# A bias product on TensorE with 128 rows of contraction, 126 of them zeros, in place of two

## The chip, the cores and the metric

The kernel runs on one core of one Trainium2 chip. The metric is the device time of one execution in microseconds (us), lower is better. A core has TensorE (PE, matrix products; its weight loads are listed apart as PEld), VectorE (DVE), ScalarE (ACT), GpSimd (POOL) and SyncE (SP). Each runs its own instruction list in order and waits for the others on semaphores.

## The reference, cut to what matters

One layer: additive attention without a score matrix, then a mixture of experts. The part that the change touches is the end of the attention:

```python
wv = (pooled_k[:, None, :, :] * mixed_q.reshape(b, s, h, dh)).reshape(b, s, dm)
return wv @ Wt + bt + mixed_q        # mixed_q = hidden_states @ Wq + bq
...
x = x + _L0_attn_ref(_layernorm(x), ...)
x = x + _L0_ffn_ref(_layernorm(x), ...)
```

There are 2 batches of 2048 tokens, and 256 features per token. Since `pooled_k` is one vector per batch, the attention's output is, for each token, `xn @ M + c`, with one 256x256 matrix `M = Wq (diag(pooled_k) Wt + I)` and one row `c` of 256 numbers for the batch.

## The kernel before

The tokens lie in `x_sb` as 32 tiles of 128 tokens. The attention's last step, here called the projection, goes over 16 pairs of tiles: `project(q)` on TensorE for q = 0 to 15 (batch 0 has q = 0 to 7, batch 1 has q = 8 to 15). Each pair has one bank of `psU`, 128 partitions by 2 x 256 numbers, and gets 13 products:

- L599, four products: the high part of the normalised input (`xhigh`, stationary) by the high part of `M` (`mhl[:, 0]`), 256 columns each
- L603, four: the low part of the input (`xlow`) by the high part of `M`
- L608, four: the high part of the input by the low part of `M`
- L611, one: the bias row `c`. It is split into a high and a low row, `cpair`, which have the partitions 0 and 1; the stationary operand `one2` is two rows of ones. So this product has 2 rows of contraction, 128 output partitions and 2 x 256 moving columns (the same row twice, by a broadcast). It closes the accumulation.

All operands of these 13 products are of type fp32r. On VectorE `add_rows(q)` waits for the product L611 of pair q, adds the bank to `x_sb` (L1261) and takes the statistics of both tiles (L1264, L1265). After every fourth pair `second_moments_of` works out a variance (L1111 to L1124), GpSimd raises it to -1/2 (`zscale`, L424), and ScalarE (the last group: VectorE, L1281) writes normalised rows to `z_sb` (L891). TensorE transposes these (`turn_z`, L621), ScalarE copies them to `xT` (L928), and from there come the router's product (L632) and the first products of the expert part (`up`, L698, L700, L704, whose operand `xhl` is made by ScalarE at L945 and VectorE at L1290). The rest of the program, from about 105 us on, is the expert part.

The order of the work is written out by hand on each engine. TensorE's list has the second batch's pooling steps between the products of batch 0 (`fold_key` L500 and L504, `score` L519, `turn_max` L526, `spread_max` L532, `turn_probs` L540, `pool_rows` L548, `project_pooled` L567), and `turn_z` between those of batch 1. VectorE's list has the answering steps between its `add_rows`; L1216 writes `gk`, which `fold_key` reads. `bias_row(b)` (L1238 to L1240) writes `cpair` for batch b, and the first `project` of a batch waits for it. `cpair` and `one2` are SBUF tensors of 2 partitions. At its start VectorE fills 256 columns of `flat` (the trace calls it fold) with ones at L1296, for TensorE's opening products L757, and then waits for the first tile of x (L1133). `helpers` makes `one2` with one copy (L1165).

Of the kernel before, what the change touches and what calls it, by code (L numbers as in the profile page):

```python
# [19 lines left out]
ALU = mybir.AluOpType  # L20
ACT = mybir.ActivationFunctionType
F32 = mybir.dt.float32
F32R = mybir.dt.float32r
# [5 lines left out]
P = 128  # L29
D, KD = 256, 2  # L30
# [3 lines left out]
B, S = 2, 2048  # L34
# [36 lines left out]
C_HILO = C_ROW + 1  # L71
# [15 lines left out]
def build(nc, x, consts, attn, norm, bt, wpack, b1pack, b2pack, out):  # L87
    with ExitStack() as ctx:
        def sb(name, shape, dt=F32):
            return ctx.enter_context(nc.sbuf_tensor(name, shape, dt))  # L90
# [4 lines left out]
        def sem(name):  # L95
            return ctx.enter_context(nc.semaphore(name))
# [11 lines left out]
        cst = sb("cst", [P, C_ALL])  # L108
# [53 lines left out]
        flat = fold[:].rearrange("p a b k d -> p (a b k d)")  # L162
# [12 lines left out]
        with ExitStack() as early:  # L175
            z_sb = early.enter_context(nc.sbuf_tensor("z_sb", [P, NT, D], F32))
            att = early.enter_context(nc.sbuf_tensor("att", [P, A_ALL], F32))
            cpair = early.enter_context(nc.sbuf_tensor("cpair", [2, B, D], F32R))
            one2 = early.enter_context(nc.sbuf_tensor("one2", [2, P], F32R))
            stats = early.enter_context(nc.sbuf_tensor("stats", [P, NT, 6], F32))  # L180
            ssum, sdif, sm2, mean, var, vare, rstd, nmr = (
                early.enter_context(nc.sbuf_tensor(name, [P, NT], F32))
                for name in ("ssum", "sdif", "sm2", "mean", "var", "vare", "rstd", "nmr"))
            gk = early.enter_context(nc.sbuf_tensor("gk", [P, KD, B, 32], F32))
            pool_sb = early.enter_context(nc.sbuf_tensor("pool_sb", [P, B, KD, NH], F32))
# [17 lines left out]
        ones = cst[:, C_ONE:C_ONE + P]  # L203
# [21 lines left out]
        crow, chi = xin[0:2, 0, 0, 0:D], xin[0:2, 0, 1, 0:D]  # L225
# [39 lines left out]
        var_ready, rstd_ready, fill_ready = sem("var_ready"), sem("rstd_ready"), sem("fill_ready")  # L265
# [193 lines left out]
        def _(pe):  # L459
            mm = nc.tensor.matmul  # L460
# [125 lines left out]
            def project(q):  # L586
                before = [p for p in range(q) if proj_bank[p] == proj_bank[q]]
                if before:
                    pe.wait_ge(x1_ready, before[-1] + 1)
                b = 2 * q // (NT // B)  # L590
                if q % (NT // 4) == 0:
                    pe.wait_ge(m_ready[b], 1)
                pair = psU[:, proj_bank[q], :].rearrange("p (t n) -> p t n", t=2)
                n = q // 2
                cols = [slice((2 * q + tt) % 4 * P, ((2 * q + tt) % 4 + 1) * P) for tt in range(2)]
                pe.wait_ge(xhigh_ready, n + 1)
                for tt in range(2):
                    for k in range(KD):
                        mm(pair[:, tt, :], xhigh[b][:, n % 4, k, cols[tt]], mhl[:, 0, k, :], start=(tt == 0 and k == 0), stop=False)  # L599
                pe.wait_ge(xlow_ready, n + 1)  # L600
                for tt in range(2):
                    for k in range(KD):
                        mm(pair[:, tt, :], xlow[:, n, k, cols[tt]], mhl[:, 0, k, :], start=False, stop=False)  # L603
                if q % (NT // 4) == 0:
                    pe.wait_ge(m_low[b], 1)
                for tt in range(2):
                    for k in range(KD):
                        mm(pair[:, tt, :], xhigh[b][:, n % 4, k, cols[tt]], mhl[:, 1, k, :], start=False, stop=False)  # L608
                if q % (NT // 4) == 0:
                    pe.wait_ge(crow_ready[b], 1)  # L610
                last = mm(pair, one2[:, :], cpair[:, b:b + 1, :].to_broadcast([2, 2, D]), start=False, stop=True)  # L611
                last.then_inc(proj_ps, 1)

            def turn_z(q):
# [182 lines left out]
            mix(0)  # L797
            turn_pooled(1, 0)
            project(0)
            project_pooled(1, 0)  # L800
            project(1)
            fold_key(1)
            project(2)
            score(1, 1)
            project(3)
# [46 lines left out]
            for r in range(2):  # L852
                pe.wait_ge(logits_sb, r + 1)
                for i in range(4):
                    last = nc.tensor.transpose(psT[:, r, i * P:(i + 1) * P], lgT[:, r, i * P:(i + 1) * P], ident)
# [241 lines left out]
        def _(dve):  # L1097
            count = [0]

            def link(ins):  # L1100

                count[0] += 1
                ins.then_inc(dve_step, 1)
                dve.wait_ge(dve_step, count[0])

            V = nc.vector
# [20 lines left out]
            def stats_of(c):  # L1127
                if c >= 2:
                    dve.wait_ge(x_loaded[c], 16)
                for t in range(c * CH, (c + 1) * CH):  # L1130
                    if c < 2:
                        dve.wait_ge(first_loaded[t], 16)
                    last = V.bn_stats(stats[:, t, :], x_sb[:, t, :])  # L1133
                return last

            def first_moments(i):
                a, z = GRP[i]
                link(stats_of(z // CH - 1))
                moments(a, z, False, var_ready)
# [19 lines left out]
            def helpers():  # L1159
                link(V.tensor_reduce(own, ident.rearrange("p (g h) -> p h g", g=4), X, ALU.add))  # L1160
                V.tensor_copy(sel.rearrange("p (g h) -> p g h", g=4),
                              own.rearrange("p (o h) -> p o h", o=1).to_broadcast([P, 4, 32]))
                for n in range(KD):
                    V.tensor_scalar(bqrep[:, n, :], ones[:, 0:32], att[:, A_BQ + n:A_BQ + n + 1], None, ALU.mult)
                V.tensor_copy(one2[:], ones[0:2, :])  # L1165

            def row_max(b, r):

# [66 lines left out]
            def bias_row(b):  # L1235

                dve.wait_ge(crow_ps[b], 1)
                link(V.tensor_tensor(crow, psD[0:2, b, 0:D], bt_bc[0:2, :], ALU.add))  # L1238
                link(V.tensor_copy(chi.bitcast(F32R), crow))
                V.scalar_tensor_tensor(cpair[:, b, :], chi, cst[0:2, C_HILO:C_HILO + 1], crow,  # L1240
                                       ALU.mult, ALU.add).then_inc(crow_ready[b], 1)

            def mix_low(b):
# [50 lines left out]
                last.then_inc(xlo_ready, 1)  # L1294

            V.memset(flat[:, 0:256], 1.0).then_inc(fill_ready, 1)  # L1296
            stats_of(0)
            first_moments(0)
            stats_of(2)
# [6 lines left out]
            folded_query()  # L1306
            first_moments(2)
            helpers()
            row_max(0, 0)
            offsets(2)  # L1310
# [28 lines left out]
            mix_low(0)  # L1339
            dve.wait_ge(bt_loaded, 16)  # L1340
            bias_row(0)
            add_groups(1, 0)
            add_rows(0)
# [22 lines left out]
            second_moments_of(1)  # L1366
            mix_low(1)
            bias_row(1)
            z_offsets(1)
            add_rows(8)  # L1370
# [407 lines left out]
```

## Time and profile before

| | us |
|---|---|
| median of 3 runs | 724.13 |
| the runs | 722.74, 725.20, 724.13 |
| time of the profiled execution | 722.72 |
| its span, first to last instruction | 720.9 |

| engine | busy us | share of the span |
|---|---|---|
| TensorE, products | 703.4 | 98% |
| TensorE, weight loads | 587.1 | 81% |
| VectorE | 574.8 | 80% |
| ScalarE | 444.5 | 62% |
| GpSimd | 183.3 | 25% |

The profiled execution is 1.4 us shorter than the median. A product's row gives when it was issued and how long it took; products overlap, so what a product takes from TensorE is read from the distance between its start and the start of the next. The sizes in a product's row, 128\*128 or 2\*128, are rows of contraction by output partitions.

### The profile page before, as it was taken

Reading aid. Unit: us, or ns where it says so; the run is one execution under the profiler, and the core shown is the slowest. Engines: PE = TensorE matmul, PEld = TensorE weight load, DVE = VectorE, ACT = ScalarE, POOL = GpSimd, SP = SyncE. Lnnn points to the kernel's source line nnn. Section 1 sums busy time; section 2 is a strip of 40 time slices with the busy share of each in tenths; the row PEclk is TensorE's granted clock in tenths of the full one; section 3 lists DMA queues with packets and bytes.
Section 4 is the critical chain, followed back from the end, with each engine's and each line's share of the span. In section 5 each row is a group of like instructions: output and inputs, shape, how many; then the busy total and the mean of one; then the engine's idle time right before and its main releaser. Section 6 shows DMA issues by size and latency. Waiting matters only on the chain.

```text
span 720.9 us, 11492 instructions
## 1 busy us (share of the span) xinstructions
PE 703.4 (98%) x4148; PEld 587.1 (81%) x4148; DVE 574.8 (80%) x1127; ACT 444.5 (62%) x745; POOL 183.3 (25%) x155
## 2 busy tenths in 40 slices
PE   8899999999999999999999999999999999999997
PEld 6547676877888988998888889988988888888886
DVE  6657887998867868896788698968877888768997
ACT  3643577437536768578658685668585775866532
POOL 1100010000003432544344343533342633121000
PEclk9999999999999999999999999999999999999999
DMA  8500122030004645754666455745654766524772
GB/s 289 223 2 1 60 92 84 1 124 2 1 1 115 217 134 181 248 177 160 208 204 224 150 167 186 250 145 179 219 158 143 198 224 195 167 81 139 249 235 100
DMA packets 46185, 106.93 MB, mean 148 GB/s; under 512 B 9421, under 2 KB 34000, under 8 KB 38576
## 3 DMA queue, kind: packets, MB, share of 16 engines
q1 hardware_dynamic: 39312, 88.49, 37.8%
q0 software_dynamic: 6816, 17.71, 7.5%
q8 instruction: 33, 0.54, 0.3%
q14 instruction: 24, 0.20, 0.1%
HBM read 89.39 MB, written 17.69 MB: 149 GB/s over the span
## 4 chain that ended last, share of the span: by engine, by line
PE 82%; DVE 11%; ACT 4%; issue 1%; POOL 1%; DMA 1%; SPq 0%; DVEq 0%; ACTq 0%
PE psD L727 24%; PE psD L733 12%; PE psU L704 11%; PE psU L700 11%; PE psU L698 11%; PE psT L648 2%; PE psU L519 1%; DVE hlo L1396 1%; ACT hid L1019 1%; PE psU L672 1%; PE psU L674 1%; PE psU L671 1%; PE psU L683 1%; PE psD L548 1%; DVE stats L1133 1%
## 5 line engine op out<-in xcount | busy, mean ns | idle before, releaser
L1019 ACT ACTIVATE hid<-psU,b 128x512 f32<-128x512 f32 (+2 forms) x280 | 152.9, 580 | 128.0 <-issue 77.8
L727 PE MATMUL psD<-w,hhi 128*128 128x512 f32 x824 | 214.0, 399 | 1.4 <-DVE x_sb L1440 0.8
L1396 DVE TENSOR_TENSOR hlo<-hid,hhi 128x512 fp32r<-128x512 f32 x206 | 138.7, 690 | 43.5 <-ACT hhi L1022 41.4
L727 PEld LDWEIGHTS psD<-w,hhi 128*128 128x128 f32 x824 | 147.5, 188 | 31.1 <-DVE x_sb L1440 1.4
L1446 DVE TENSOR_TENSOR w<-raw,w 128x1024 fp32r<-128x1024 f32 x112 | 133.4, 1219 | 2.1 <-ACT w L897 1.6
L431 POOL DMA_INDIRECT xin<-token_in,src x71 | 79.4, 1118 | 209.8 <-DVE src L1642 106.3
L439 POOL DMA_INDIRECT token_out<-fold,dst x71 | 89.6, 1261 | 168.1 <-DVE fold L1440 162.2
L704 PE MATMUL psU<-xhl,w 128*128 128x512 f32 (+1 forms) x448 | 124.7, 360 | 0.1
L698 PE MATMUL psU<-xhl,w 128*128 128x512 f32 (+1 forms) x448 | 124.5, 359 | 0.2 <-ACT xhl L945 0.2
L700 PE MATMUL psU<-xhl,w 128*128 128x512 f32 (+1 forms) x448 | 124.2, 358 | 0.0
L733 PEld LDWEIGHTS psD<-w,hlo 128*128 128x128 f32 x824 | 111.2, 188 | 10.7 <-DVE hlo L1396 1.3
L733 PE MATMUL psD<-w,hlo 128*128 128x256 f32 x824 | 114.8, 279 | 0.5 <-DVE hlo L1396 0.4
L897 ACT ACTIVATE w<-raw 128x1024 fp32r<-128x1024 f32 x104 | 103.2, 1064 | 13.2 <-DMA raw<-in_wpack 13.2
L1022 ACT ACTIVATE hhi<-psU,b 128x512 fp32r<-128x512 f32 x150 | 102.6, 684 | 0.0
L704 PEld LDWEIGHTS psU<-xhl,w 128*128 128x128 f32 x448 | 79.3, 188 | 13.5 <-DVE xhl L1290 0.5
L700 PEld LDWEIGHTS psU<-xhl,w 128*128 128x128 f32 x448 | 79.4, 188 | 12.8
L698 PEld LDWEIGHTS psU<-xhl,w 128*128 128x128 f32 x448 | 77.5, 188 | 12.3 <-ACT hhi L1022 0.4
L1438 DVE TENSOR_TENSOR fold<-psD,b 128x256 f32<-128x256 f32 x71 | 29.9, 421 | 22.8 <-issue 21.1
L1392 DVE CAST hhi<-hid 128x512 fp32r<-128x512 f32 x56 | 23.8, 425 | 27.1 <-ACT hid L1019 26.2
L1440 DVE TENSOR_TENSOR fold<-psD,fold 128x256 f32<-128x256 f32 x71 | 30.1, 424 | 2.4
L1014 ACT ACTIVATE hid<-psU 128x512 f32<-128x512 f32 x14 | 8.4, 599 | 34.8 <-issue 29.6
L1292 DVE SCALAR_TENSOR_TENSOR xhl<-psT,nw,xhl 128x512 fp32r<-128x512 f32 (+2 forms) x54 | 28.1, 562 | 1.9 <-ACT xhl L949 1.0
(221 smaller groups left out, 640.6 us busy)
## 6 DMA issues: line engine op xcount, KB each, us to landing
raw<-in_wpack SPq DMA_DIRECT2D x58, 1024.0 KB
xT<-token_out SPq DMA_DIRECT2D x32, 256.0 KB, 3.2
token_in<-z_sb SPq DMA_DIRECT2D x8, 512.0 KB, 2.9
out<-x_sb SPq DMA_DIRECT2D x16, 256.0 KB, 3.4
b<-in_b2pack SPq DMA_DIRECT2D x29, 128.0 KB
x_sb<-in_x SPq DMA_DIRECT2D x6, 512.0 KB, 8.1
xin<-token_in,src POOLq DMA_INDIRECT x71
token_out<-fold,dst POOLq DMA_INDIRECT x71
```

The lines of the kernel that those rows point to most:

```text
L431: nc.gpsimd.indirect_dma_start(xin[:, j % 2, q, :], None, zs, bass.IndirectOffsetOnAxis(src[:, y:y + 1], 0)).then_inc(xin_loaded[j % 2], 16)
L439: nc.gpsimd.indirect_dma_start(ys, bass.IndirectOffsetOnAxis(dst[:, y:y + 1], 0), yo[:, n % 4, :], None, bounds_check=2 * T - 1, oob_is_er ...
L698: mm(acc, whi[slot][:, cols[k]], xhl[:, k, 0, 0:rows], start=(k == 0), stop=False)
L700: mm(acc, wlo[slot][:, cols[k]], xhl[:, k, 0, 0:rows], start=False, stop=False)
L704: last = mm(acc, whi[slot][:, cols[k]], xhl[:, k, 1, 0:rows], start=False, stop=(k == KD - 1))
L727: mm(acc, hhi[:, part], wpair[slot][:, :, c * D:(c + 1) * D], start=(c == 0), stop=False)
L733: return mm(acc[:, 1, :], hlo[:, part], whi[slot][:, c * D:(c + 1) * D], start=False, stop=(c == MH - 1))
L897: nc.scalar.activation(whi[slot][:, half], raw[:, h, half], copy).then_inc(w_hi[h], 1)
L1019: last = nc.scalar.activation(hid[:, n % 4, i * rows:(i + 1) * rows], acc, ACT.Relu, bias=b1[:, u % 2, m:m + 1])
L1022: last = nc.scalar.activation(hhi[:, j * 512:(j + 1) * 512], acc, ACT.Relu, bias=b1[:, u % 2, m:m + 1])
L1396: V.tensor_tensor(hlo[:, part], hid[:, n % 4, :], hhi[:, part].bitcast(F32), ALU.subtract).then_inc(hlo_ready, 1)
L1446: last = V.tensor_tensor(wlo[slot][:, half], raw[:, h, half], whi[slot][:, half].bitcast(F32), ALU.subtract)
```

## The change

`cpair` and `one2` become tensors of 128 partitions. `one2` is all ones. `cpair` is filled with zeros at VectorE's start (the ones of `flat` times 0, two instructions of 128x256, behind a wait for the fill at L1296), and `bias_row` then writes its partitions 0 and 1 as before. The product L611 takes all 128 partitions: 128 rows of contraction, of which 126 add zero.

```diff
-            cpair = early.enter_context(nc.sbuf_tensor("cpair", [2, B, D], F32R))
-            one2 = early.enter_context(nc.sbuf_tensor("one2", [2, P], F32R))
+            cpair = early.enter_context(nc.sbuf_tensor("cpair", [P, B, D], F32R))
+            one2 = early.enter_context(nc.sbuf_tensor("one2", [P, P], F32R))
...
-                last = mm(pair, one2[:, :], cpair[:, b:b + 1, :].to_broadcast([2, 2, D]), start=False, stop=True)
+                last = mm(pair, one2[:, :], cpair[:, b:b + 1, :].to_broadcast([P, 2, D]), start=False, stop=True)
...
-                V.tensor_copy(one2[:], ones[0:2, :])
+                V.tensor_copy(one2[:], ones)
...
-                V.scalar_tensor_tensor(cpair[:, b, :], chi, cst[0:2, C_HILO:C_HILO + 1], crow,
+                V.scalar_tensor_tensor(cpair[0:2, b, :], chi, cst[0:2, C_HILO:C_HILO + 1], crow,
...
             V.memset(flat[:, 0:256], 1.0).then_inc(fill_ready, 1)
+            dve.wait_ge(fill_ready, 1)
+            for b in range(B):
+                V.tensor_scalar(cpair[:, b, :], flat[:, 0:D], 0.0, None, ALU.mult)
```

The number of instructions and their order are the same on TensorE, ScalarE, GpSimd and SyncE. On VectorE two are new; this is the start of its list, and the place of the copy in `helpers` (from that start on, lines of the changed kernel are three higher):

```order
 L1296 MEMSET fold 128x256
+L1299 TENSOR_SCALAR cpair<-fold 128x256 x2
 L1133 BN_STATS stats<-x_sb 128x6 x8
 L1111 TENSOR_TENSOR ssum<-stats 128x8
@@ -36,5 +37,5 @@
 L1161 COPY posm<-posm 128x128
 L1164 TENSOR_SCALAR xin<-cst,att 128x32 x2
-L1165 CAST one<-cst 2x128
+L1165 CAST one<-cst 128x128
 L1170 TENSOR_REDUCE small<-psU 128x1
```

The zero fill stands between the fill of `flat` and the first statistics of x; the copy keeps its place and writes 128 partitions.

## Rows read from the trace of the kernel before

**Rows 1.** Page: busy time of two engines, the chain that ended last, TensorE's clock.

```profile
PE 703.4 (98%) x4148; PEld 587.1 (81%) x4148; DVE 574.8 (80%) x1127; ACT 444.5 (62%) x745; POOL 183.3 (25%) x155
...
PEclk9999999999999999999999999999999999999999
...
PE 82%; DVE 11%; ACT 4%; issue 1%; POOL 1%; DMA 1%; SPq 0%; DVEq 0%; ACTq 0%
```

**Rows 2.** Lines L611, L608: weight loads, ns min/median/max; who waited (us, times).

```profile
L611 PEld LDWEIGHTS psU<-cpair,one x16: 181/181/182, 56.2 to 104.0; 2*128 2x128 f32 x16
...
  DVE x_sb L1261: 5.2, 7
...
L608 PEld LDWEIGHTS psU<-mhl,w x64: 186/188/189, 55.5 to 103.7; 128*128 128x128 f32 x64
```

**Rows 3.** Timeline, TensorE around the product of pair 10: start us, length us, what.

```profile
92.45 0.28 PE L608 MATMUL psU<-mhl,w 128*128 128x256 f32 x1
92.67 0.50 PE L611 MATMUL psU<-cpair,one 2*128 2x512 f32 x1
93.09 0.33 PE L621 MATMUL psT<-cst,z_sb 128*128 128x128 f32 x1
```

**Rows 4.** The same, where a 512-column product of 128 rows precedes such transposes.

```profile
109.69 0.39 PE L704 MATMUL psU<-xhl,w 128*128 128x512 f32 x1
109.92 0.27 PE L621 MATMUL psT<-cst,z_sb 128*128 128x128 f32 x1
```

**Rows 5.** The same, where the output partitions go from 128 to 32 and back.

```profile
83.47 0.59 PE L576 MATMUL psU<-fold,att 128*128 128x256 f32 x2
...
83.69 0.38 PE L576 MATMUL psU<-fold,att 128*128 128x256 f32 x1
83.99 0.40 PE L580 MATMUL psD<-fold,xin 128*32 128x256 f32 x1
...
84.97 0.33 PE L621 MATMUL psT<-cst,z_sb 128*128 128x128 f32 x1
```

**Rows 6.** The chain of waits, 84 to 150 us, in order: start us, share us, what.

```profile
91.79 0.47 PE psU L603 x4
...
95.16 0.44 PE psU L611
...
98.58 2.56 POOL zscale L424
...
109.35 0.73 PE psU L704 x2
```

**Rows 7.** Timeline, VectorE between the products of batch 0; idle before in brackets.

```profile
58.90 0.39 DVE L1216 TENSOR_SCALAR gk<-att,pq 128x32 f32<-128x32 f32 x2
...
67.28 0.69 DVE L1261 TENSOR_TENSOR x_sb<-psU,x_sb 128x512 f32<-128x512 f32 x1 [1.24 <-PE psU L611]
```

**Rows 8.** Timeline, VectorE from the second `cpair` to pair 11.

```profile
87.14 0.47 DVE L1240 SCALAR_TENSOR_TENSOR cpair<-xin,cst 2x256 fp32r<-2x256 f32 x1
...
88.19 0.69 DVE L1261 TENSOR_TENSOR x_sb<-psU,x_sb 128x512 f32<-128x512 f32 x1 [0.41 <-PE psU L611]
...
95.70 0.69 DVE L1261 TENSOR_TENSOR x_sb<-psU,x_sb 128x512 f32<-128x512 f32 x1 [0.73 <-PE psU L611]
```

**Rows 9.** Timeline, VectorE's start, and the durations (ns) of lines L1165 and L1161.

```profile
2.94 0.85 DVE L1133 BATCH_NORM_STATS2 stats<-x_sb 128x6 f32<-128x256 f32 x2 [1.82 <-DMA x_sb<-in_x]
...
10.84 1.70 DVE L1149 TENSOR_SCALAR z_sb<-x_sb,mean,rstd 128x256 f32<-128x256 f32 x5
...
L1165 DVE CAST one<-cst x1: 207/207/207, 21.6 to 21.6; 2x128 fp32r<-2x128 f32 x1
...
L1161 DVE COPY posm<-posm x1: 229/229/229, 21.1 to 21.1; 128x128 f32<-128x128 f32 x1
```

**Rows 10.** Timeline, TensorE at the router's two products L632.

```profile
105.01 0.64 PE L632 MATMUL psD<-xT,posm 128*32 128x512 f32 x4 [0.49 <-ACT xT L928]
...
118.24 0.64 PE L632 MATMUL psD<-xT,posm 128*32 128x512 f32 x4 [1.37 <-ACT xT L928]
```

## The prediction, made before the changed kernel was run

> **What bounds the kernel now.** I read the page first. TensorE is busy for 98% of the span and is 82% of the chain that ended last, at the full granted clock in all 40 slices [rows 1]. So time taken off TensorE should reach the end, unless the stretch where it is taken off is held by another engine. All 16 bias products start between 56.2 and 104.0 us [rows 2], so next I read the chain of waits there. From 56 to 76 us it is TensorE's own work almost without a break. From 78 to 87.6 us it goes through ScalarE and VectorE (the second batch's pooling result, up to `cpair` at L1240 [rows 8]). From there to 95.16 it is TensorE again; then it leaves through L611 and VectorE's add for GpSimd, ScalarE and VectorE, and comes back to TensorE only with L704 at 109.35 [rows 6]. Behind that the expert part runs at TensorE's pace.
>
> Then I read single products. The reader should see the distances between starts. Four products of 256 columns take 0.47, so 0.118 each (L603 [rows 6]). Around L611 it looks different [rows 3]: 0.21 to 0.22 from the last L608 to L611, and 0.43 from L611 to the transpose behind it. A product of 512 columns with 128 rows before the same transposes takes 0.23 [rows 4]. And the first transpose behind L611 takes 0.33, where behind L704 it takes 0.27 [rows 3, 4].
>
> **What the 2-row form costs, per product.** 0.09 to 0.10 ahead of it (0.21 - 0.118), 0.20 in its own place (0.43 - 0.23), 0.06 behind it: 0.35. Where a 256-column product stands behind it the last term is 0.10, by the same excess as that of L611's own length (0.50 against 0.39 for L704). Is this due to the 2 rows? The trace has another change of shape with the same marks: going from 128 output partitions to 32 the distance is 0.30 for a 256-column product (L576 to L580) whose usual distance is 0.21 (two last 0.59, one 0.38), and coming back the first transpose again takes 0.33 [rows 5]. The excess of 0.09 and the lengthened first product are those of L611. So I take it that TensorE runs L611 in another arrangement of its array, finishes what it has before it changes, and can't load the weights ahead across the change. With 128 rows the shape is that of its neighbours, and a distance of 0.23 with no excess is what [rows 4] shows.
>
> The Trainium skill, TensorEngine Tiling, Key Properties, says the same: "Changing tiling mode (not just tile) drains the TensorE". A rule of its TensorE page speaks against the change and is a rival below.
>
> TensorE's ceiling would be 16 x 0.35 to 0.39, some 6 us. Not all comes, since four of the products have a change of shape behind them anyway or wait for another engine.
>
> **Batch 0, pairs 0 to 7.**
> - Pair 0: L611 started within 0.1 of the end of `cpair`, so at most 0.09 comes ahead of it, its own weights are not loaded early, and it gives 0.28 behind.
> - Pair 1: `fold_key` (L500) behind it needs `gk`, which VectorE ends at 59.29 [rows 7] after the add of pair 0, and that add comes 0.09 earlier only. So L500 starts 0.3 earlier, not 0.7. Sum 0.31.
> - Pair 2: 0.09 ahead. Behind it is `score` (32 output partitions), so a change of shape stays; its price is 0.09 by [rows 5], hence 0.43 becomes 0.32: 0.11. Sum 0.51.
> - Pair 3: 0.09 ahead, and 0.11 for its own weights, now loaded early. It ends 0.71 earlier, and VectorE, which waits for it (idle 1.24 before the add at 67.28 [rows 7]), starts 0.71 earlier.
> - From here TensorE could go on to gain (pairs 4 to 6 have 0.1 to 0.3 each), but the softmax steps in between wait for VectorE's and ScalarE's list, which runs without a gap behind that add. So what reaches `cpair` at 87.14 is VectorE's 0.71. Pair 7 gives nothing: `mix(1)` behind it waits for VectorE.
>
> **Batch 1, pairs 8 to 15.** The product of pair 8 starts with the end of `cpair` (87.61), 0.71 earlier, and then gives 0.15 (0.09 and 0.06; its own load stays exposed). Pair 9 gives 0 further, as the transposes behind it wait for rows that ScalarE writes; these came 0.15 earlier too. Pair 10 gives its full 0.35 and pair 11 0.20 up to its end (0.09 and 0.11). TensorE ends pair 11 by 0.71 + 0.15 + 0.35 + 0.20 = 1.4 earlier. VectorE is busy without a gap from 88.19 to 94.97 (the adds and statistics of pairs 8 to 10 and two halves of a weight split), then idle for 0.73 until the add of pair 11 [rows 8]. Moved by 0.71 it is free at 94.26, so this add can start at 94.29 and not before: 95.70 - 94.29 = 1.41. Both sides agree on **1.4 us**.
>
> From here the chain is variance, `zscale` on GpSimd, `z_sb` and `xT` on ScalarE, `xhl`, and L704 [rows 6]. TensorE's further gain (pairs 12 to 15, to some 2.8 us in all at 104 us) only makes it wait longer for ScalarE before the router's product at 105.01. The third `zscale` and the last add are not on this chain. So L704 at 109.35, and all behind it, starts 1.4 earlier, and nothing there depends on absolute time: the expert weights are asked for when the routing is done.
>
> **What is added.** Two VectorE instructions of 128x256. The nearest rows are 0.34 each (L1149, five in 1.70 us, 128x256 [rows 9]) and 0.47 (L1240, 2x256, two inputs [rows 8]). They start with the end of the fill, at 1.12, and end by 1.8 to 2.1; the first tile of x comes at 2.94, and VectorE is idle for 1.82 before it [rows 9]. Cost nothing; without that cover 0.7 to 0.95. TensorE's opening products are released by the fill itself, which is ahead. The copy at L1165 took 0.207 with 2 partitions, a copy of 128x128 took 0.229 [rows 9]: 0.02 at most, at 21.6 us, where VectorE's step is not waited for. A weight load of 128 rows took 0.188 (L608), one of 2 rows 0.181 [rows 2]: hidden under the product before, 0 to 0.007.
>
> Sum: 722.72 - 1.4 = 721.3 for the profiled execution, span 719.5. It lay 1.4 below the median; from the median, 724.13 - 1.4 = **722.7 us**, 0.2% faster. A measurement of this kernel can tell about 0.3% (2.2 us) from no change, so this would count as the same.
>
> **The rivals.**
> 1. **The rows of contraction cost and save nothing** (the distances belong to something else in L611, such as its broadcast operand). Then only the VectorE instructions are new: 724.1. For it speaks that no other product of few rows with 128 output partitions is in the trace; against it, the equal excess in [rows 5]. The Trainium skill, TensorE: Matmul & The Clock Gate, in its table of advice, says that a matmul with 32 rows takes the same time as one with 128; by that rule this is the result. The product alone may well obey it; [rows 3] shows the cost at its two edges. Chance 0.15.
> 2. **Half of it**: the change of shape goes, but the weights of L611 or of its successor still aren't loaded ahead. Then 0.10 to 0.2 less per product, and VectorE's add of pair 3 comes some 0.35 earlier, that of pair 11 0.7: 723.4. Chance 0.12.
> 3. **The path is freed more**: TensorE's 2.8 us at the end of pair 15 count, because ScalarE's or VectorE's waits that I hold for binding shorten too. 724.13 - 2.8 = 721.3; the ceiling is 724.1 - 6. Against it: VectorE's list has no gap from 88.19 to 94.97. Chance 0.08.
> 4. **Slower: TensorE falls idle and loses its clock.** It would end pair 15 2.8 earlier, and the router's product comes 1.4 earlier; the idle time of 0.49 before it at 105.01 [rows 10] becomes 1.9 us. The longest in this stretch today is 1.37 (before 118.24), with the clock at full speed [rows 1]. If the longer one brought 1.2 GHz in place of 2.4, TensorE's pieces of the chain behind it, 6 to 7 us between 109.35 and 116.02, could double: 724.1 - 1.4 + 2 to 6.7 = 725 to 729. It decides when an idle time beyond 1.37 is enough to lower the clock. Chance 0.05.
>
> **How the numbers follow.** My forecast, 1.4 us, has 0.60; the rivals 0.15, 0.12, 0.08 and 0.05. The runs of before lie 1.4 below and 1.1 above their median, so a true 1.4 may be measured as more than 2.2 in about one case of five: 0.12 of faster, with rival 3 0.20. Slower by over 0.3% is rival 4, 0.05. The rest, 0.75, is within 0.3%. Range: from rival 3 less a little scatter, 720.9, to rival 1 with scatter, 724.5.
>
> **What would show it.** In the profile after: L611 with a length near 0.39, starting 0.12 behind the last L608, and its successor 0.23 behind it; the first transposes at 0.27. L500 only 0.3 earlier. The add of pair 3 at 66.6, `cpair` at 86.4, the add of pair 11 at 94.3 with almost no idle time before it, L704 at 107.9, a span of 719.5. If L611 keeps its distance of 0.43, rival 1 holds. If VectorE waits before pair 11's add by more than 0.1, a step of TensorE is mis-sized. If the clock has a slice below 9 after 103 us, rival 4.

## The result, and the profile after

| | before | changed |
|---|---|---|
| median of 8 runs, us | 723.21 | 721.52 |
| time of the profiled execution | 722.72 | 721.32 |
| its span | 720.9 | 719.5 |

The ratio is 0.9971, with a 95% interval of 0.9957 to 0.9984: 2.1 us faster, between 1.2 and 3.1 (the two medians of the table differ by 1.7). The forecast was 722.7 us, 1.4 us faster. The engines' clock and the split of the work are as before; TensorE is busy for 3.9 us less. From the page (busy time, then the share of the chain), to be held against [rows 1]:

```profile
PE 699.5 (97%) x4148; PEld 586.1 (81%) x4148; DVE 575.3 (80%) x1129; ACT 444.2 (62%) x745; POOL 181.8 (25%) x155
...
PE 79%; DVE 12%; ACT 5%; issue 2%; POOL 1%; DMA 1%; SPq 0%; DVEq 0%; ACTq 0%
```

**The product.** Line L611 of the changed kernel (ns min/median/max, then who waited for it, us and times), against [rows 2], and TensorE's timeline around the product of pair 10 (start us, length us), against [rows 3]:

```profile
L611 PE MATMUL psU<-cpair,one x16: 391/397/498, 56.4 to 101.3; 128*128 128x512 f32 x16
...
  DVE x_sb L1261: 3.2, 4
```

```profile
91.29 0.64 PE L608 MATMUL psU<-mhl,w 128*128 128x256 f32 x4
91.76 0.40 PE L611 MATMUL psU<-cpair,one 128*128 128x512 f32 x1
92.00 0.27 PE L621 MATMUL psT<-cst,z_sb 128*128 128x128 f32 x1
```

The four L608 take 0.64 and one takes 0.28, so the last starts at 91.65 and L611 0.11 behind it, in place of 0.21. Its successor starts 0.24 behind it, in place of 0.43, and takes 0.27 in place of 0.33. The length of L611 fell from 0.50 to 0.40.

The weight loads (PEld) show where the distances come from. Here are those of L611 and of the product behind it in pair 14, before and then in the changed kernel:

```profile
101.98 0.18 PEld L611 LDWEIGHTS psU<-cpair,one 2*128 2x128 f32 x1
102.41 0.53 PEld L599 LDWEIGHTS psU<-mhl,w 128*128 128x128 f32 x4 [0.25 <-issue]
```

```profile
99.56 0.19 PEld L611 LDWEIGHTS psU<-cpair,one 128*128 128x128 f32 x1
99.68 0.66 PEld L599 LDWEIGHTS psU<-mhl,w 128*128 128x128 f32 x4
```

Before, both loads started together with their products (101.98 and 102.41), so none was done ahead. In the changed kernel the products start at 99.67 and 99.91, 0.11 and 0.23 behind their loads.

**Where the gain arrives.** First the chain of waits between 84 and 150 us, against [rows 6], then VectorE's timeline, against [rows 7, 8]:

```profile
94.36 0.70 DVE x_sb L1261
...
97.24 2.56 POOL zscale L424
...
108.01 0.74 PE psU L704 x2
```

```profile
66.80 0.69 DVE L1261 TENSOR_TENSOR x_sb<-psU,x_sb 128x512 f32<-128x512 f32 x1 [1.00 <-PE psU L611]
...
86.47 0.47 DVE L1240 SCALAR_TENSOR_TENSOR cpair<-xin,cst 2x256 fp32r<-2x256 f32 x1
...
93.90 0.41 DVE L1265 BATCH_NORM_STATS2 stats<-x_sb 128x6 f32<-128x256 f32 x1
94.36 0.69 DVE L1261 TENSOR_TENSOR x_sb<-psU,x_sb 128x512 f32<-128x512 f32 x1
```

The add of pair 3 comes 0.48 earlier, the second `cpair` 0.67, the add of pair 11 1.34, the third `zscale` and L704 1.34. The idle time ahead of the add of pair 11 (0.73 before) is gone. In the chain, TensorE has given way to VectorE between 87 and 94 us.

**The ruler for the experiments.** The first product of the projection is the first start of L599; from the same row of each run, with its span, one gets how long the kernel takes from there to its end:

```profile
L599 PE MATMUL psU<-mhl,w x64: 276/279/388, 54.9 to 100.3; 128*128 128x256 f32 x64
```

This is 719.5 - 54.9 = 664.6 us here, against 720.9 - 54.7 = 666.2 before (the same row there has "54.7 to 102.9"). So the part that the change can reach became 1.6 us shorter, and the part ahead of it was 0.27 longer in this execution. The second is scatter, as the experiments show, and the table at their end gives both numbers for each kernel.

**What was added.** The two instructions of the zero fill, and what VectorE waited for behind them, against [rows 9]:

```profile
1.16 0.49 DVE L1299 TENSOR_SCALAR cpair<-fold 128x256 fp32r<-128x256 f32 x2
2.93 0.77 DVE L1133 BATCH_NORM_STATS2 stats<-x_sb 128x6 f32<-128x256 f32 x2 [1.27 <-DMA x_sb<-in_x]
```

They end at 1.65, and the first tile of x comes at 2.93 as before.

### The profile page after: what moved, and what is told of

Same layout as the page of the kernel before. It is cut to its first block, busy times and chain, and to the rows that moved or that the text cites. A ratio compares the mean times of both kernels' runs of the same rounds, so it can differ in the third digit from the quotient of the medians.

```text
span 719.5 us, 11494 instructions
## 1 busy us (share of the span) xinstructions
PE 699.5 (97%) x4148; PEld 586.1 (81%) x4148; DVE 575.3 (80%) x1129; ACT 444.2 (62%) x745; POOL 181.8 (25%) x155
## 4 chain that ended last, share of the span: by engine, by line
PE 79%; DVE 12%; ACT 5%; issue 2%; POOL 1%; DMA 1%; SPq 0%; DVEq 0%; ACTq 0%
PE psD L727 24%; PE psD L733 12%; PE psU L704 11%; PE psU L700 11%; PE psU L698 11%; PE psT L648 2%; ACT z_sb L891 1%; PE psU L519 1%; DVE hlo L1399 1%; ACT hid L1019 1%; PE psU L672 1%; PE psU L674 1%; PE psU L671 1%; PE psU L683 1%; DVE stats L1133 1%
## 5 line engine op out<-in xcount | busy, mean ns | idle before, releaser
L439 POOL DMA_INDIRECT token_out<-fold,dst x71 | 88.1, 1241 | 169.5 <-DVE fold L1443 163.7
L704 PE MATMUL psU<-xhl,w 128*128 128x512 f32 (+1 forms) x448 | 124.7, 360 | 0.1
L704 PEld LDWEIGHTS psU<-xhl,w 128*128 128x128 f32 x448 | 79.3, 188 | 13.5 <-DVE xhl L1290 0.5
```

Source lines behind the costliest of these rows:

```text
L439: nc.gpsimd.indirect_dma_start(ys, bass.IndirectOffsetOnAxis(dst[:, y:y + 1], 0), yo[:, n % 4, :], None, bounds_check=2 * T - 1, oob_is_er ...
L704: last = mm(acc, whi[slot][:, cols[k]], xhl[:, k, 1, 0:rows], start=False, stop=(k == KD - 1))
```

## The experiments

### Is it the rows of the product? (e1 to e4)

The four kernels have all of the change but the number of partitions that the product takes: 2, 32, 64 or 96.

```diff
-                last = mm(pair, one2[:, :], cpair[:, b:b + 1, :].to_broadcast([P, 2, D]), start=False, stop=True)
+                last = mm(pair, one2[0:2, :], cpair[0:2, b:b + 1, :].to_broadcast([2, 2, D]), start=False, stop=True)
```

> Everything of the change but the product itself: both operands have 128 partitions and the zero fill stands at VectorE's start, but the product takes partitions 0 and 1 only, as before. My theory (the cost lies in the change of shape around a product of few rows): the time of before within 0.05%, L611 again 0.43 us ahead of its successor, and the add of pair 11 with 0.7 us of idle time before it. Rival (the fill, or the operands' placing, made the gain or moved the input stage by the 0.26 us that the profile of after shows at 17 us): 1 to 2 us faster than before in the first case; the start of the first zscale stretch 0.3 us later in the second.

> The product takes 32 rows of contraction, 30 of them zeros. If the number of rows that carry data mattered, or the time grew with the rows, L611 would lie between. My theory, with the array arranged in strips: 32 rows are the same arrangement as 2, so L611 starts 0.21 us behind the last L608 and its successor 0.43 behind it, as before; span near 720.9 us. Rival (rows as such): a distance clearly below 0.43.

> 64 rows of contraction. My theory: half an array is still another arrangement than the neighbours' 128 rows; distances 0.21 and 0.43 us as with 2 rows, L611's own length near 0.50, span near 720.9. Rival (only strips of 32 are an arrangement of their own): 0.12 and 0.23 us, length 0.39, span 719.5.

> 96 rows of contraction. If what counts is the smallest of 32, 64 and 128 rows that holds the product, 96 rows count as 128: distances 0.12 and 0.23 us, length 0.39, span near 719.5. Rival (anything that is not all 128 rows is a change): 0.21 and 0.43 us, span near 720.9.

With 2 rows the median was 723.30 us, ratio to before 1.0001 (0.9987 to 1.0016): the rest of the change neither costs nor saves. The rows of L611 with 2, 32, 64 and 96 rows, one line of each kernel:

```profile
L611 PE MATMUL psU<-cpair,one x16: 496/497/500, 56.8 to 104.6; 2*128 2x512 f32 x16
```

```profile
L611 PE MATMUL psU<-cpair,one x16: 496/497/500, 58.7 to 106.5; 32*128 32x512 f32 x16
```

```profile
L611 PE MATMUL psU<-cpair,one x16: 498/501/502, 57.5 to 105.4; 64*128 64x512 f32 x16
```

```profile
L611 PE MATMUL psU<-cpair,one x16: 392/394/499, 58.4 to 103.4; 96*128 96x512 f32 x16
```

With 2, 32 and 64 rows its median length is 0.50 us, and from the first of the 16 to the last it takes 47.8 or 47.9 us, as before (56.2 to 104.0). With 96 rows it is 0.39, and 45.0 us, as with 128 (56.4 to 101.3: 44.9). From the first L599 to the end: 666.1, 666.3, 666.3, and 664.7 with 96 rows. So what costs is that the product's arrangement is not its neighbours', and a product of 96 rows has theirs. The distances with 32 rows are 0.22 ahead and 0.43 behind, with 64 rows 0.21 and 0.44, as expected. Whether 64 rows and 32 are one arrangement or two isn't told by these runs. The expected spans of e2, e3 and e4 (720.9, 720.9 and 719.5) were missed, 723.4, 722.2 and 721.6, since the part ahead of the projection took longer; see below.

Could few rows cost by themselves, whatever stands beside them? The trace of the kernel before has eight product instructions of 1 row and 32 output partitions behind one another (L532, 69.21). The product behind them starts at 69.56, so all eight with the edge behind them take 0.35, less than one L611 of 2 rows (0.43):

```profile
69.21 0.42 PE L532 MATMUL psD<-cst,mrow 1*32 1x128 f32 x8
```

### What the change of shape costs by itself (e5, e6)

```diff
+                    mm(acc[:, 1, :], ones[0:2, :], cst[0:2, C_EYE + P:C_EYE + 3 * P], start=False, stop=False)
                     for c in range(early, MH):
                         last = rest(c)
```

This is e6; e5 has `0:128` in place of `0:2`.

> The changed kernel with one more product in each of the 103 row blocks of the expert part's down step (between the L727 and the L733 products): ones by zeros, 128 rows of contraction, 256 columns, type f32, which adds zero. An f32 product of 256 columns goes as two instructions of 0.216 us (L576). With 128 rows there is no change of shape, so my theory gives 103 x 0.43 = 44.5 us more than the changed kernel, some 764 to 766 us. It is the base for the next run.

> The same 103 added products, with 2 rows of contraction. My theory (a change of shape costs 0.09 us ahead, 0.20 in its place and 0.10 behind): 0.39 us each more than with 128 rows, so 40 us more than the run with 128 rows, some 804 to 808 us. Rival (the distances of the projection are a matter of that product's broadcast operand or of its place, not of the rows): the same time as with 128 rows within 2 us.

763.93 and 805.34 us. From the first L599 to the end it took 706.4 and 749.3: 42.9 us more with 2 rows, for 103 products, so 0.42 us for each (0.39 expected). The added products with 128 rows took 41.8 us more than none, 0.41 each (0.43 expected). About 1.0 of these 41.8 is the clock's: from the third `zscale` to the first L704 it takes 11.79 us in e5 (98.10 to 109.89), and 10.76 in e6 (96.56 to 107.32). So the price of a change of shape is 0.42 to 0.43 for each of these f32 products. The row of the added product in e5, then in e6:

```profile
L745 PE MATMUL psD<-cst x206: 377/378/382, 129.2 to 757.2; 128*128 128x256 f32 x103
```

```profile
L745 PE MATMUL psD<-cst x206: 374/426/479, 126.8 to 798.4; 2*128 2x256 f32 x103
```

Each product is two instructions. With 2 rows one of the two takes 0.48 and the other 0.37, where with 128 both take 0.38: the 0.10 of a load that isn't done ahead (the weight loader is idle for 0.35 ahead of each of these 103 pairs, 35.7 us in all). The rest of the 0.42 lies at the edges. The rival that blamed the broadcast operand or the place in the program falls: this product has no broadcast, is f32, and stands in another part. Each of e2 to e7 and e10 is a single execution.

### Is TensorE the limit in this stretch? (e7, e10)

e7 is the changed kernel without the bias product; its output lacks the bias row.

```diff
-                if q % (NT // 4) == 0:
-                    pe.wait_ge(crow_ready[b], 1)
-                last = mm(pair, one2[:, :], cpair[:, b:b + 1, :].to_broadcast([P, 2, D]), start=False, stop=True)
```

> The changed kernel without the 16 bias products (the bias row isn't added, so the output lacks it); VectorE still makes the row. TensorE saves another 16 x 0.23 = 3.7 us. If TensorE alone set the pace here, as a rival has it, the stretch from the first product of the projection to the end would be 3 us or more shorter than in the changed kernel. My theory: VectorE's list, without a gap from the add of pair 8 to that of pair 11, holds it, and can start only some 0.5 us earlier because pair 8 no longer waits for the row's end; so 0.5 to 0.9 us less than the changed kernel.

It was 664.3, only 0.3 less than in the changed kernel, below both. The add of pair 11 was 1.3 us earlier, more than I had given it, and the third `zscale` as well. So 1.0 us was lost behind them. TensorE's timeline at the router's product, and the granted clock in four stretches (stretch, length, TensorE busy with its count, clock, DMA share, GB/s):

```profile
104.43 3.21 PE L629 MATMUL psD<-xT,posm 128*32 128x512 f32 x16 [3.70 <-ACT xT L925]
```

```profile
102.00:104.00 2.00, 0.00 (x0) 1.00 0.04 12
104.00:106.00 2.00, 1.57 (x12) 0.73 0.73 250
106.00:108.00 2.00, 2.00 (x10) 0.50 0.33 115
108.00:110.00 2.00, 2.00 (x13) 0.92 0.43 147
```

TensorE was idle for 3.70 us ahead of the router's product. Its clock then fell from 2.4 to 1.2 GHz (1.00 to 0.50 in the rows), and the 16 instructions took 3.21 us in place of 1.92. This is my fourth rival, in a kernel that makes TensorE still earlier. The same happened in e5, whose projection is that of the changed kernel and whose idle time was that of the changed kernel too:

```profile
104.53 3.30 PE L632 MATMUL psD<-xT,posm 128*32 128x512 f32 x16 [1.95 <-ACT xT L929]
```

```profile
105.00:107.00 2.00, 2.00 (x16) 0.50 0.28 94
```

So at 1.95 us of idle time the clock can fall and need not: it did in e5, it did not in the profiled executions of the changed kernel, of e4 and of e6. e10 is e7 with five filler products between the last projection and the router.

```diff
             project(15)
+            busy(psD[:, 1, 0:256], 5)
             router(0)
```

> The changed kernel without the 16 bias products, and with five filler products (f32, 256 columns, 0.43 us each, result not used) on TensorE between project(15) and the router. Without the fillers TensorE was idle for 3.70 us before the router's product, its clock was granted at half speed from 104.9 to 108.3 us, and of the 1.3 us by which the add of pair 11 and the third zscale came earlier only 0.3 reached the end. My theory (the clock took the other 1.0): idle time some 1.5 us, full clock from 56 us on, and from the first product of the projection to the end 663.3 us, 1.3 less than in the changed kernel. Rival (another wait behind took it): 664.3 whatever the clock.

```profile
100.28 2.32 PE L465 MATMUL psD<-cst 128*128 128x256 f32 x10
104.16 1.92 PE L629 MATMUL psD<-xT,posm 128*32 128x512 f32 x16 [1.55 <-ACT xT L926]
```

```profile
104.00:106.00 2.00, 1.84 (x16) 1.00 0.59 201
```

The clock stays full, the router's instructions take 1.92 again, and the time from the first L599 is 663.3, as expected: 1.0 less than e7, though TensorE has more to do. The clock took that 1.0 us: from the third `zscale` to the first L704 it takes 11.77 us in e7 and 10.76 in e10. And with the 16 products gone altogether, 1.3 us is all that this stretch gives; TensorE's pairs behind the eleventh count for nothing.

### The collision on GpSimd (e8, e9)

In the changed kernel, as before, the third `zscale` takes 2.55 us and the others 1.64. It starts 0.16 us behind VectorE's weight split `first_lo(1, 0)` (97.24 and 97.08 in the changed kernel). e8 moves this split behind `z_offsets(2)`, e9 beside its other half:

```diff
             second_moments_of(2)
-            first_lo(1, 0)
             add_rows(12)
             z_offsets(2)
...
             lows(0, 0, 4)
+            first_lo(1, 0)
             first_lo(1, 1)
```

> The changed kernel with VectorE's weight split first_lo(1, 0) (L1191, 1.22 us) moved from ahead of add_rows(12) to behind z_offsets(2). In the changed kernel GpSimd's third-stretch zscale (L424) takes 2.56 us where it runs beside that split, and 1.64 in the other stretches; it is on the chain. My theory: it takes 1.64 now, and L704 and all behind come 0.9 us earlier: 0.997 x 0.9987, ratio to before 0.9958, some 720.4 us. Rival (the length belongs to the data or to this place, not to the split beside it): 2.56 stays, and the ratio is that of the changed kernel.

721.02 us, ratio 0.9971 (0.9957 to 0.9984). The expected 0.9958 lies inside the interval, and so does the rival's; the profile tells them apart: the third `zscale` took 1.64, but 664.0 from the first L599 is 0.6 less than in the changed kernel, not 0.9. GpSimd in e8, and below in e9:

```profile
98.97 1.64 POOL L424 TENSOR_TENSOR zscale<-vare,posm 128x8 f32<-128x8 f32 x1 [10.32 <-DVE vare L1124]
107.83 2.02 POOL L424 TENSOR_TENSOR zscale<-vare,posm 128x8 f32<-128x8 f32 x1 [7.23 <-DVE vare L1124]
```

> The changed kernel with VectorE's split first_lo(1, 0) moved behind the expert part's first four low parts, beside its other half first_lo(1, 1), where VectorE is idle for over 2 us. With the split behind z_offsets(2), GpSimd's third zscale took 1.64 us in place of 2.55, but the end moved by 0.6 us only: the split then delayed the last adds by 0.24, and the fourth zscale, beside L1290, took 2.02. My theory: without the split there, all four zscales take 1.64, and from the first product of the projection to the end it takes 0.9 us less than in the changed kernel (664.6), so 663.7. Rival (another step behind is late next): 664.0 or more, as with the earlier place.

```profile
96.84 1.64 POOL L424 TENSOR_TENSOR zscale<-vare,posm 128x8 f32<-128x8 f32 x1 [10.33 <-DVE vare L1124]
104.56 1.64 POOL L424 TENSOR_TENSOR zscale<-vare,posm 128x8 f32<-128x8 f32 x1 [6.08 <-DVE vare L1124]
```

In e8 VectorE is late next. From the split at 100.88 its list has no gap through the last adds and the variance to L1290, so L704 starts 52.4 us behind the first L599, against 53.1 in the changed kernel: 0.7 earlier and not 0.9, and 0.6 reached the end. The fourth `zscale` took 2.02 there, but it isn't on that chain. In e9 both are short, and the time from the first L599 is 718.1 - 54.5 = 663.6, 1.0 less than in the changed kernel (663.7 expected). The end to end measurement, 721.32 us with a ratio of 0.9971 (0.9956 to 0.9987), doesn't show it: its 12 runs lie in two groups, 719.4 to 720.3 and 722.3 to 723.4.

Running beside VectorE's work is not enough to lengthen a `zscale`. The fourth one and L1290, first in the kernel before, then VectorE's row in e8:

```profile
107.52 1.64 POOL L424 TENSOR_TENSOR zscale<-vare,posm 128x8 f32<-128x8 f32 x1 [6.38 <-DVE vare L1124]
108.00 1.29 DVE L1290 TENSOR_TENSOR xhl<-xT,xhl 128x512 fp32r<-128x512 f32 x2 [0.57 <-ACT xhl L945]
```

```profile
107.67 1.29 DVE L1290 TENSOR_TENSOR xhl<-xT,xhl 128x512 fp32r<-128x512 f32 x2
```

Before, L1290 started 0.48 us after the `zscale` and ran beside the rest of it, and the `zscale` still took 1.64; so it did in e9, where L1290 started 0.78 after it (105.34). In e8 L1290 was already running when the `zscale` began (107.67 and 107.83). The third `zscale` of the changed kernel ended 1.50 us behind the end of the split that ran when it began (98.30 and 99.80), and the fourth of e8 1.50 behind the end of the first of the two L1290 (108.35 and 109.85). So what lengthened it was the instruction already running.

### Where the scatter comes from (e11, e12)

Both add five filler products on TensorE in gaps of the input stage, e11 to e9's kernel, e12 to the kernel before:

```diff
             fold_query()
+            busy(psU[:, 3, 0:256], 3)
             for q in range(4, 8):
                 turn_rows(q)
+                if q == 5:
+                    busy(psU[:, 3, 0:256], 1)
+            busy(psU[:, 3, 0:256], 1)
             score(0, 0)
```

> The kernel with the split moved beside its other half, and five filler products on TensorE in gaps of the input stage (three before turn_rows(4), one after turn_rows(5), one before score(0, 0)). In six of ten profiles the granted clock fell to a half for some microseconds between 19 and 31 us, and the first product of the projection then started up to 3 us later, while the stretch behind it was the same within 0.1 us. My theory: with the fillers the clock does not fall there, the first product of the projection starts near 54.2 to 55.3 us, and the runs lie closer together; ratio to before some 0.995. Rival (the clock falls whatever TensorE does there, or the fillers delay the transposes): the first product at 56 us or later, and a ratio as without the fillers.

The count in this expectation is wrong: of the ten profiles up to then five had the low clock between 19 and 31 us; a sixth, e5, had it at 105 us. The granted clock in e2, the profile with the latest start of the projection (columns as above), and then in e12:

```profile
18.00:20.00 2.00, 1.61 (x14) 0.92 1.05 425
20.00:22.00 2.00, 1.22 (x8) 0.50 0.98 382
```

```profile
18.00:20.00 2.00, 2.00 (x17) 1.00 1.00 400
20.00:22.00 2.00, 1.65 (x17) 1.00 1.00 397
```

Ahead of the fall TensorE had been idle for 1.67 us and then had a gap of 0.39 between its transposes (e2, TensorE's timeline), and this was so too in kernels whose clock stayed full, as e9:

```profile
17.72 1.12 PE L478 MATMUL psT<-cst,z_sb 128*128 128x128 f32 x8 [1.67 <-DVE z_sb L1149]
19.23 1.57 PE L478 MATMUL psT<-cst,z_sb 128*128 128x128 f32 x8 [0.39 <-ACT xT L878]
```

```profile
17.28 1.12 PE L478 MATMUL psT<-cst,z_sb 128*128 128x128 f32 x8 [1.67 <-DVE z_sb L1149]
18.79 1.11 PE L478 MATMUL psT<-cst,z_sb 128*128 128x128 f32 x8 [0.39 <-ACT xT L878]
```

e11 has a median of 720.17 us over 6 runs, all between 719.76 and 720.80, ratio 0.9955 (0.9939 to 0.9971).

> The kernel before, with its product of 2 rows, and only the five filler products in the gaps of the input stage. The runs of before lie in two groups, 722.4 to 723.6 and 724.8 to 726.0 us. My theory (the upper group are executions in which TensorE's clock is granted at half for some microseconds between 19 and 31 us): the upper group goes, all runs lie within 1.5 us of each other near 722.0 to 723.2, the ratio to before is 0.998 to 0.9995, and from the first product of the projection to the end it takes the 666.2 us of before. Rival (the spread has another cause, and the good spacing of the earlier run was chance): two groups again, 2 us apart.

722.87 us, ratio 0.9993 (0.998 to 1.0007). Eleven of the 12 runs lie between 721.92 and 723.32, one at 724.33; of the 16 runs of the kernel before beside them four lie at 725.4. The upper group is gone but for that one, and the low runs are where they were. The expectation that all runs lie within 1.5 us of each other was missed by that one (2.4). The fillers' effect on the median alone isn't clear of the measurement.

Each run has its mean granted clock on record, and that names the groups. Of the 67 runs of the kernel before that were made beside the experiments, 44 have a clock of 0.999 or 1.000 and take 721.8 to 724.0 us (median 722.8), and 17 have 0.994 or 0.995 and take 724.6 to 726.0 (median 725.3). The six with 0.998 take 723.8 to 724.7. The run of e12 at 724.33 has 0.998. e9's two groups are six runs at 0.999 or 1.000 and six at 0.994 or 0.995.

All profiles together. "Low clock" is the stretch in which the granted clock was at a half, outside the last 3 us:

| kernel | first L599, us | from there to the end | low clock |
|---|---|---|---|
| before | 54.7 | 666.2 | none |
| changed | 54.9 | 664.6 | none |
| e1, 2 rows | 55.2 | 666.1 | none |
| e2, 32 rows | 57.1 | 666.3 | from 19.7 |
| e3, 64 rows | 55.9 | 666.3 | from 26.8 |
| e4, 96 rows | 56.9 | 664.7 | from 18.7 |
| e5, extra with 128 rows | 55.7 | 706.4 | from 104.9 |
| e6, extra with 2 rows | 54.2 | 749.3 | none |
| e7, no product | 57.0 | 664.3 | from 19.6, from 104.9 |
| e8, split later | 56.6 | 664.0 | from 27.3 |
| e9, split with its half | 54.5 | 663.6 | none |
| e10, no product, filled | 56.7 | 663.3 | from 19.3 |
| e11, e9 and fillers | 54.3 | 663.8 | none |
| e12, before and fillers | 54.9 | 666.2 | none |

The start of the projection is 54.2 to 55.7 without the early low clock and 55.9 to 57.1 with it, some 2 us later in the middle (54.8 and 56.8). The time behind it agrees within 0.2 us between kernels of the same shape.

## Why the prediction was right, point by point

- **The product's anatomy.** Forecast 0.12, 0.23 and a first transpose of 0.27; measured 0.11, 0.24 and 0.27. e2 to e4 show that the number of rows decides only by the arrangement it brings, and e6 prices the change at 0.42 us in a stretch where TensorE sets the pace. Rival 1 is excluded by e1 and e6, rival 2 by L611's own row and by the weight loads.
- **Pairs 0 to 3.** Forecast 0.71 at the add of pair 3. Measured 0.48, and 0.75 once the later start of the projection (0.27) is taken off. `fold_key` (L500) started at 59.51 against 59.56, so 0.32 earlier on that scale; forecast 0.3.
- **From pair 3 to `cpair`: a step that failed.** I held that only VectorE's 0.71 reaches `cpair`. Measured 0.67 + 0.27 = 0.94. The mistake is at ScalarE's L928 at 76.94: I took it to follow ScalarE's own rows, but those rows could have let it start some 0.2 earlier (the last three L891 take 1.57 and one takes 0.59, so they start 0.49 apart, the last at 76.25, and the next could start at 76.74), and it waited for TensorE's transposes: the chain of waits before has `76.41 0.45 PE psT L621 x4` and then `76.94 0.47 ACT xT L928`. With TensorE earlier it starts at 76.28, 0.66 earlier, where the ScalarE work ahead moved by 0.47. ScalarE's timeline before, then after:

```profile
75.27 1.57 ACT L891 ACTIVATE z_sb<-x_sb,nmr,zscale 128x256 f32<-128x256 f32 x3
76.94 0.47 ACT L928 ACTIVATE xT<-psT,nw 128x256 f32<-128x256 f32 x1
```

```profile
74.80 1.57 ACT L891 ACTIVATE z_sb<-x_sb,nmr,zscale 128x256 f32<-128x256 f32 x3
76.28 0.84 ACT L928 ACTIVATE xT<-psT,nw 128x256 f32<-128x256 f32 x2
```

- **Pairs 8 to 11.** Forecast 1.41 at the add of pair 11, with VectorE's list as the limit. Measured 1.34 + 0.27 = 1.61, with the idle time of 0.73 gone. The difference is the 0.2 above; the gain within this stretch was 0.70 forecast and 0.67 measured.
- **Behind it.** All of it reaches the end: 666.2 - 664.6 = 1.6. The prediction's sentence that the third `zscale` is not on this chain is a slip: [rows 6], which it quotes, has it there with 2.56 us, and so has the changed kernel (97.24). The fourth is the one off the chain. The sum doesn't change by it.
- **The size.** 1.4 was forecast, and 1.6 is what the reachable part gave. That the span of 719.5 was met to the last digit is luck: 0.2 us too little gain and 0.27 us of a late start cancel. The measured 2.1 (1.2 to 3.1) holds both, and since its interval leaves out 0, a gain of 0.3% could be told from none here.
- **Rival 3** (TensorE's further gain counts) is excluded by e10: with every product gone, 1.3 us more at most. TensorE was 2.7 earlier at pair 15 (101.32 against 104.02), 3.0 with the late start taken off, where 2.8 was forecast, and waited.
- **Rival 4** (idle TensorE loses its clock). The idle time became 1.95 us as forecast (1.9). In the profiled execution the clock stayed full, in e5's it fell with the same idle time. So the mechanism is real in some executions of this kernel. Its price was mis-sized: 1.0 us between L632 and L704 (e7 against e10, e5 against e6), not 2 to 6.7, since only the router's product and some transposes fall into the low stretch, and part of that isn't on the chain.
- **Added work.** No cost: e1 has the ratio 1.0001, the zero fill ended at 1.65, sooner than the 1.8 to 2.1 forecast, and the copy of `one2` took 0.218 us in place of 0.207.

## What to carry to other kernels

A matmul of few rows between matmuls of full shape costs more than its own length shows: that was 0.10 longer here, and the distances around it gave 0.35. Look at the starts and weight loads of its neighbours, and pad its operands with zeros if they can lie ready (96 of 128 rows were enough here, 64 were not). Then follow the gain to the engine that waits for it: of 16 x 0.35 to 0.39 us on TensorE 1.6 reached the end, since VectorE's and ScalarE's lists held the rest. And where TensorE is made to wait longer, look at the granted clock behind the wait, for the clock can take most of the gain: 1.0 of 1.3 us in e7, which five filler products gave back (e10).

The fastest kernel of this study is e11, with the full-row product, the split moved beside its other half, and five fillers: 720.17 us, ratio to before 0.9955 (0.9939 to 0.9971). Its six runs (719.8 to 720.8) lie near e9's six with the full clock (719.4 to 720.3), so what the fillers bring is that the upper group is absent.

## What the runs showed of the hardware that I had not expected

- TensorE's granted clock fell from 2.4 to 1.2 GHz behind gaps that in other executions of the same instructions left it at 2.4: behind 1.95 us of idle time once in four profiles, and in the input stage in six of the twelve profiles without fillers there, from 19 or from 27 us on. With it the projection started some 2 us later, and the runs with the lower mean clock (0.994 or 0.995) took 2.5 us longer in the kernel before. With the gaps filled, none of two profiles had it, and 17 of 18 runs lay in the lower group. Why one execution has it and the next does not stays open.
- GpSimd's `tensor_tensor` of 128x8 took 1.64 us, but 2.55 when VectorE had begun a 128x1024 `tensor_tensor` from SBUF to SBUF (L1191, 1.22 us) 0.16 us before it, and 2.02 when it had begun L1290 0.16 before it (e8). Where L1290 began 0.48 or 0.78 us after it, it took 1.64 (the kernel before, e9). The Trainium skill, GPSIMD Engine Reference, 1. Specifications, lists SBUF interfaces that GpSimd shares with VectorE, with contention from VectorE instructions that have two SBUF inputs; both L1191 and L1290 have two, and the traces agree where such an instruction was already running, but not where it began later.
